# Attention with experts on one core: two heads stacked and normalised ahead of one output product of 128 rows

## The reference

```python
normed = x / l2 * dim ** 0.5 * gamma
q, k, v = split_heads(normed @ w_qkv)             # 16 heads of 64
sim = einsum('bhid,bhjd->bhij', q * d ** -0.5, k)
sim = where(causal_mask, -max, sim)
attn = softmax(sim, axis=-1)
out = einsum('bhij,bhjd->bhid', attn, v)          # (b, h, 1024, 64)
return concat_heads(out) @ w_out                  # (1024, 1024) @ (1024, 128)
```

## Time and profile before

| | |
|---|---|
| median of 3 runs | 1565.51 us (1565.09 to 1565.91) |
| the profiled execution | 1564.66 us, of which the span of the instructions is 1562.8 us |
| granted TensorE clock, mean | 0.969 of 2.4 GHz; 1.00 through the attention from 340 us to 1500 us |
| busy over the span | PE 93%, DVE 69%, ACT 68%, POOL 58% |
| 500 to 1500 us, per 200 us | PE 195 to 197, DVE 143 to 153, ACT 147 to 149, POOL 133 to 140 |

### The profile page before, as it was taken

One profiled execution on the slowest core, in us unless ns is written; L12 is line 12 of the kernel. 1 busy time (PEld: TensorE's weight loads), 2 busy tenths in 40 slices (PEclk: granted clock), 3 DMA queues, 4 the chain that ended last, 5 costly groups with the idle time before them and its releaser, 6 DMA issues.

```text
span 1562.8 us, 28739 instructions
## 1 busy us (share of the span) xinstructions
PE 1449.6 (93%) x9130; PEld 1126.8 (72%) x9131; DVE 1076.4 (69%) x2341; ACT 1067.4 (68%) x2590; POOL 907.1 (58%) x923
## 2 busy tenths in 40 slices
PE   3559999699999999999999999999999999999998
PEld 3548888467777777777777777777777777777776
DVE  6565555457776877687768776876687668866883
ACT  2445566267777777777777777777777777777775
POOL 0762000157666766676667666766676667666766
PEclk9579999689999999999999999999999999999999
DMA  9122211111111111111111111111111111111111
GB/s 311 46 79 71 58 54 52 44 35 42 33 28 38 40 33 29 38 40 33 29 38 40 33 28 40 38 33 28 39 38 33 28 41 37 33 28 42 37 28 55
DMA packets 58759, 72.34 MB, mean 46 GB/s; under 512 B 7400, under 2 KB 44560, under 8 KB 58640
## 3 DMA queue, kind: packets, MB, share of 16 engines
q1 hardware_dynamic: 40720, 52.57, 14.2%
q10 hardware_dynamic: 13824, 9.86, 2.0%
q0 software_dynamic: 4096, 8.40, 1.8%
HBM read 20.47 MB, written 16.52 MB: 24 GB/s over the span
## 4 chain that ended last, share of the span: by engine, by line
PE 66%; DVE 9%; ACT 3%; issue 2%; DMA 1%; SPq 0%; POOLq 0%; POOL 0%; DVEq 0%; ACTq 0%
PE max_ps L1291 9%; PE score_ps L1316 8%; PE score_ps L1317 8%; PE misc_ps L1350 8%; PE head_ps L1333 7%; PE head_ps L1337 7%; PE head_ps L1335 7%; PE misc_ps L1267 3%; DVE q_a L1125 3%; PE max_ps L1294 2%; PE score_ps L1319 2%; DVE row_max L1135 2%; ACT p_hi L1082 1%; PE misc_ps L1261 1%; PE misc_ps L1300 1%
## 5 line engine op out<-in xcount | busy, mean ns | idle before, releaser
L1033 POOL TENSOR_TENSOR p_lo<-probs,p_hi 128x512 fp32r<-128x512 f32 (+3 forms) x768 | 775.0, 1025 | 415.1 <-ACT p_hi L1082 408.7
L1082 ACT ACTIVATE probs<-score_ps 128x512 f32<-128x512 f32 (+3 forms) x768 | 375.4, 489 | 236.2 <-PE score_ps L1319 168.6
L1135 DVE TENSOR_REDUCE row_max<-max_ps 128x1 f32<-128x128 f32 (+7 forms) x512 | 386.7, 756 | 157.2 <-PE max_ps L1294 146.7
L1082 ACT ACTIVATE p_hi<-score_ps 128x512 fp32r<-128x512 f32 (+3 forms) x768 | 373.2, 486 | 0.0
L1333 PE MATMUL head_ps<-p_hi,v_hi 128*65 128x512 f32 (+3 forms) x768 | 295.2, 384 | 0.3 <-POOL p_lo L1033 0.3
L1316 PE MATMUL score_ps<-q_a,k_a 128*128 128x512 f32 (+3 forms) x768 | 266.6, 347 | 3.1 <-DMA q_b<-shift 3.1
L1317 PE MATMUL score_ps<-q_b,k_b 65*128 65x512 f32 (+3 forms) x768 | 266.9, 348 | 0.0
L1291 PE MATMUL max_ps<-k_a,q_a 128*128 128x384 f32 (+5 forms) x768 | 249.6, 380 | 16.4 <-DVE row_max L1135 12.6
L1337 PE MATMUL head_ps<-p_lo,v_hi 128*65 128x512 f32 (+3 forms) x768 | 258.7, 337 | 0.0
L1335 PE MATMUL head_ps<-p_hi,v_lo 128*64 128x512 f32 (+3 forms) x768 | 258.5, 337 | 0.0
L1316 PEld LDWEIGHTS score_ps<-q_a,k_a 128*128 128x128 f32 x768 | 144.8, 189 | 46.4 <-issue 3.7
(11 more groups left out here) (170 smaller groups left out, 2106.0 us busy)
## 6 DMA issues: line engine op xcount, KB each, us to landing
k_a<-k_a SPq DMA_DIRECT2D x64, 256.0 KB, 3.3
q_b<-q_a SPq DMA_DIRECT2D x64, 256.0 KB, 4.2
sorted_x<-zeros SPq DMA_DIRECT2D x13, 384.0 KB, 15.2
w_raw<-sorted_x SPq DMA_DIRECT2D x26, 192.0 KB, 2.5
sorted_y<-result ACTq DMA_DIRECT2D x78, 64.0 KB, 1.6
acc<-in_L_attn_x_dram SPq DMA_DIRECT2D x4, 512.0 KB, 9.0
w_raw<-in_L_ffn_W_dram ACTq DMA_DIRECT2D x1, 2048.0 KB, 22.7
q_b<-shift SPq DMA_DIRECT2D x128, 2.0 KB
```

The lines of the kernel that those rows point to most:

```text
L1033: pool.tensor_tensor(p_lo[:, slot, 0:w], probs[:, slot, 0:w], p_hi[:, slot, 0:w].bitcast(F32), ALU.subtract).then_inc(p_split, 1)
L1082: ins = act.activation(p[:, (g * CH + c) % RING, 0:width], score_ps[(g * CH + c) % 2][:, 0:width], ACT.Exp, scale=SCALE)
L1135: dve.tensor_reduce(row_max[:, g % 2, t:t + 1], src, axes, ALU.max).then_inc(max_taken, 1)
```

## The change

The two heads of a pair share one output product. ScalarE copies each half head, still unnormalised, with its denominator row to `raw`, which holds four half heads (two heads by two halves). The denominators, 512 numbers on one partition, go through a chain of steps, whose place is counted in chunks after the half's last chunk (`CHAIN`): SP folds them to 16 partitions by 32 (a DMA, 5 chunks later), VectorE inverts (8), SP stores the inverse to DRAM (9) and spreads it from there over 64 partitions (12), VectorE multiplies `raw` with it into rows 0 to 63 or 64 to 127 of `heads` (16). The output product then has 128 rows and 128 columns, 4 tiles to a unit, two units for a pair: at chunk 8 of the even head and chunk 4 of the odd head that follow. One addition on VectorE takes a unit to `acc`. `probs` goes from 6 slots to 4, and ScalarE waits for GpSimd's step of 4 chunks before. The walk is now one list without the split by `hp`; both programs are unrolled.

```diff
-            heads = sb(ph2, "heads", [HEAD + 1, 2, SEQ])
+            raw = sb(ph2, "raw", [HEAD + 1, 2, 2, BANK])
+            heads = sb(ph2, "heads", [P, SEQ])
-            wo = sb(ph2, "wo", [HEAD + 1, 2, D + 1])
+            wo = sb(ph2, "wo", [P, D])
+            CHAIN = [("fold", 5), ("invert", 8), ("store", 9), ("spread", 12), ("normalise", 16)]
-            Y_AT = [6, 9, 10]
-            y_units = [(0, 3), (3, 3), (6, 2)]
+            Y_AT = {8: 0, CH + 4: 1}
...
+                for kind, lag in CHAIN:
+                    if at >= lag and (at - lag) // CH < ALL_HEADS and (at - lag) % CH in LAST:
+                        order.append((kind, (at - lag) // CH, LAST.index((at - lag) % CH)))
...
+                    def fold_denominator(g, half):
+                        sp.wait_ge(raw_out, n_half(g, half) + 1)
+                        sp.dma_start(den[:, half], raw[HEAD:HEAD + 1, g % 2, half].rearrange("o (f n) -> o f n", f=FOLD)
+                                     ).then_inc(den_folded[half], 16)
+                    def store_inverse(g, half):
+                        sp.wait_ge(inverted, n_half(g, half) + 1)
+                        sp.dma_start(inv_rows[half].rearrange("(f n) -> f n", f=FOLD), inv[:, half]
+                                     ).then_inc(inv_stored[half], 16)
+                    def spread_inverse(g, half):
+                        sp.wait_ge(inv_stored[half], 16 * g + 16)
+                        sp.dma_start(scale[:, half], inv_rows[half].partition_broadcast(HEAD)
+                                     ).then_inc(scale_spread[half], 16)
...
+                            if n_chunk(g, c) >= PROBS:
+                                act.wait_ge(p_split, n_chunk(g, c) - PROBS + 1)
...
-                    def denominators(hp, g, n, u):
-                        dve.reciprocal(rden[:, u % 2, 0:tiles], src[:, :, D]).then_inc(recip_done, 1)
-                    def add_y(hp, g, n, u):
-                        for t in range(tiles):
-                            ins = dve.scalar_tensor_tensor(out=row, in0=src[:, t, 0:D], scalar=rden[:, u % 2, t:t + 1],
-                                                           in1=row, op0=ALU.mult, op1=ALU.add)
+                    def invert(g, half):
+                        dve.wait_ge(den_folded[half], 16 * g + 16)
+                        dve.reciprocal(inv[:, half], den[:, half]).then_inc(inverted, 1)
+                    def normalise(g, half):
+                        dve.wait_ge(scale_spread[half], 16 * g + 16)
+                        dve.tensor_tensor(heads[s * HEAD:(s + 1) * HEAD, cols], raw[0:HEAD, s, half], scale[:, half],
+                                          ALU.mult).then_inc(normalised, 1)
+                    def add_y(p, n, u):
+                        dve.tensor_tensor(acc[:, toks], misc_ps[u % 2][:].rearrange("p (t d) -> p t d", t=GROUP),
+                                          acc[:, toks], ALU.add).then_inc(y_added, 1)
...
-                        for t in range(tiles):
-                            ins = pe.matmul(dst[:, t * (D + 1):(t + 1) * (D + 1)], heads[:, g % 2, q0:q0 + P],
-                                            wo[:, g % 2], start=True, stop=True)
+                        pe.wait_ge(normalised, n_half(2 * p + 1, n) + 1)
+                        for t in range(GROUP):
+                            ins = pe.matmul(dst[:, t * D:(t + 1) * D], heads[:, q0:q0 + P], wo[:],
+                                            start=True, stop=True)
```

More of the change, by code:

```diff
@@ L887, in numbered @@
                 return out_
-            def misc_units(order):
-                return [o[:3] for o in order if o[0] in MISC_KINDS]
-            before_loop = ([(kind, 0, n) for n in range(6) for kind in ("project", "project_lo")]
-                           + [("max", 0, m) for m in range(PARTS)]
-                           + [("shift", 0, 0)])
-            for c in range(CUT):
-                before_loop += beside(0, c, False)
-            before_loop = numbered(before_loop, 0)
-            first_units = misc_units(before_loop)
@@ L899, in attention_and_experts @@
-            MISC0 = len(first_units)
-            def plan(last):
-                order = []
-                for at in range(CUT, G * CH + (LAG if last else CUT)):
-                    order += beside(at // CH, at % CH, last)
-                if last:
-                    order += [(kind, G - 1, n) for n in range(len(y_units)) for kind in ("y", "add")]
-                return numbered(order, MISC0)
-            MISC = len(misc_units(plan(False)))
-            assert MISC % 2 == 0
-            def n_max(hp, g, m):
-                return hp * (G * PARTS) + (g * PARTS + m)
@@ L917, in n_chunk @@
[L917 to L937 removed]
+            order = [(kind, 0, n) for n in range(6) for kind in ("project", "project_lo")]
@@ new lines, in attention_and_experts, with n_max, n_chunk, n_half @@
+            order += [("max", 0, m) for m in range(PARTS)] + [("shift", 0, 0)]
+            for at in range(ALL_HEADS * CH + 2 * CH):
+                order += beside(at)
+            order = numbered(order)
+            misc_units = [o[:3] for o in order if o[0] in MISC_KINDS]
+            def n_max(g, m):
+                return g * PARTS + m
+            def n_chunk(g, c):
+                return g * CH + c
+            def n_half(g, half):
+                return g * 2 + half
+            def n_y(p, n):
+                return p * 2 + n
@@ L994, in _ @@
-                    run(walk, sp)
+                    for kind, g, c, u in order:
+                        if kind == "shift":
+                            lay_shift(g, c)
+                        elif kind == "project" and c == 3:
+                            copies(g)
+                        elif kind == "project" and c == 5 and g % BATCH == BATCH - 1 and g + 1 < ALL_PAIRS:
+                            sp.wait_ge(misc_ready, u + 1)
+                            qkv_weights(sp, g // BATCH + 1)
+                        elif kind == "gather" and g == 0:
+                            sp.wait_ge(group_taken, c + 1)
+                            sp.dma_start(x_row[:], x_tiles[:, c * GROUP:(c + 1) * GROUP]).then_inc(x_again, 16)
+                        elif kind == "fold":
+                            fold_denominator(g, c)
+                        elif kind == "store":
+                            store_inverse(g, c)
+                        elif kind == "spread":
+                            spread_inverse(g, c)
+                        elif kind == "y" and c == 1 and g % BATCH == BATCH - 1 and g + 1 < ALL_PAIRS:
+                            sp.wait_ge(misc_ready, u + 1)
+                            out_weights(g // BATCH + 1)
@@ L1228, in _ @@
-                    run(walk, dve)
+                    for kind, g, c, u in order:
+                        if kind == "max":
+                            maximum(g, c)
+                        elif kind == "project_lo":
+                            project(g, c, u)
+                        elif kind == "weights":
+                            w_lo(c)
+                        elif kind == "invert":
+                            invert(g, c)
+                        elif kind == "normalise":
+                            normalise(g, c)
+                        elif kind == "add":
+                            add_y(g, c, u)
+                        elif kind == "gather" and g == 0:
+                            dve.tensor_copy(places[:].rearrange("p (n q) -> p n q", n=2),
+                                            slots[:, :, c * GROUP:(c + 1) * GROUP]).then_inc(group_taken, 1)
+                        elif kind == "combine":
+                            combine(c, g)
@@ new lines, in _ @@
+                    for kind, g, c, u in order:
+                        if kind == "score":
+                            score(g, c)
+                        elif kind == "max":
+                            max_scores_of(g, c)
+                        elif kind == "project":
+                            project(g, c, u)
+                        elif kind == "shift":
+                            shifts(g, c, u)
+                        elif kind == "pv":
+                            values(g, c)
+                        elif kind == "y":
+                            project_out(g, c, u)
```

344 lines of the change are left out of this document (133 added, 211 removed).

## The result

The changed kernel takes 1664.79 us (median of 4, 1664.51 to 1665.60), the one before 1565.30 beside it: a ratio of 1.064 (1.062 to 1.066), 99.5 us slower. The direction was forecast, the size was not: 1573 with a range to 1598.

What follows compares the result with a forecast made beforehand. TensorE was taken to bound the attention. Eight groups of heads gave +3.6 us and the kernel's end +4.3, together +8: 1572.5 against the profiled 1564.66, 1573.4 against the median; forecast 1573, 8-in-10 range 1538 to 1598.

Steps and rivals of the forecast that it cites:

- heads with the experts' rows: Three heads of eight in attention: VectorE is full and sets the pace; its balance of work lengthens each by 0.56 us.
- The fourth rival: Even heads: the multiply loses its turn to a second GpSimd instruction, +0.69 in three heads a group, 17 us: 1590; no separate chance.
- The group's other heads: Heads without the experts' rows, two odd and three even of eight: -0.78 us for each odd, +0.11 for each even.
- The output product: TensorE in attention: units of 1.90 us replace 3.88 a pair, 1.98 off, 63 us for 32 pairs if nothing replaces them.
- the wait of 0.39 for the maximum: Even head, chunk 8: TensorE arrives earlier and waits 0.39 us until VectorE has taken the maximum before.
- Multiply, inversion, transfers: VectorE's multiply 0.56 us plus about 0.45 waiting for GpSimd, inversion 0.35; transfers: fold 1.73, store 1.6, spread 2.3.
- The second rival: Attention: the normalising multiply does not wait for GpSimd; 28 us less, 4 more after attention: about 1542; chance 0.22.
- The third rival: Even head: the fold, late behind copies, delays VectorE's inversion and next maxima; a 5 us trip gives 1611; chance 0.17.
- The end: From ScalarE's last copy to the last store's issue: 8.8 us instead of 4.5, so +4.3.
- the last unit: Final output product on TensorE, after the last multiply: priced at 0.95 us.

## Why the prediction was wrong

**The step that failed: heads with the experts' rows.** The prediction said that there "VectorE sets the pace, and its balance is" +0.56 a head. These heads lengthened by 6.46, 0.92 and 4.29 us. Yet VectorE's busy time in them, waits for GpSimd included, rose by only 1.7, 1.5 and 1.5. Head 3 before and after (columns as in the earlier trace rows):

```profile
843.85:864.64 20.79, 19.55 (x122) 14.31 (x119) 18.65 (x46) 13.94 (x33) 13.28 (x14) 1.00 0.00 1
```

```profile
878.88:906.13 27.25, 21.99 (x114) 15.97 (x112) 20.38 (x42) 13.98 (x33) 14.46 (x15) 0.87 0.04 11
```

So what failed was to take VectorE's balance for the length of the head: VectorE is idle for 6.9 us of head 3 now, and for 2.1 before. The length comes from a chain: VectorE waits for GpSimd ahead of a maximum or a multiply that TensorE needs, TensorE stands still for up to 3.82 us and then works at the 1.2 GHz level, and VectorE waits for TensorE's next product. The balance counted VectorE's own new and lost work and half a GpSimd instruction for each multiply (head 3's took 1.70 and 1.50, not 1.01). It left out that `combine`'s old instructions wait for GpSimd too, and that GpSimd's rests would go when TensorE lost the units between its chunks. The rows were there. A multiply of `combine` took 1.13 beside GpSimd; it was used to price the new instruction and not asked of the old ones. And the window in which VectorE looked full holds a copy that takes 0.16 us with GpSimd's work cut:

```profile
843.29 1.25 DVE L1146 COPY gsc<-weights 128x8 f32<-128x8 f32 x1
```

The fourth rival had the mechanism (a turn lost to a second GpSimd instruction), but in the even heads and as the upper side of the forecast, 17 us.

**The clock was not priced.** All of the earlier trace rows stood at 1.00, and a wait was counted as long as it lasts. Waits of 2.7 and 3.8 us were followed by 3.4 and 5.1 us of work at the 1.2 GHz level.

**The group's other heads.** The output product was mis-sized: from start to start it falls from 1.71 to 0.89 us a head, 0.82 and not 0.99 (the chain of waits gives each stretch to one instruction and so counted its edges). Of the wait of 0.39 for the maximum 0.07 appeared; the unit waited 0.49 for the multiply instead of 0.71. The errors cancel, so that the sums came out near by luck: +0.2 for +0.11, -0.66 for -0.78. Head 2, with its gathers, was counted as free and lost 1.0.

**Multiply, inversion, transfers.** 0.94 came for 0.56 + 0.45, 0.33 for 0.35. The second rival (no waiting) is out: alone the multiply takes 0.67. The row that it rested on shows a wait as well, on the other engine: the subtraction beside the addition of 744.62 took 1.86 us instead of 1.29.

```profile
744.60 1.86 POOL L1033 TENSOR_TENSOR p_lo<-probs,p_hi 128x512 fp32r<-128x512 f32 x1 [0.79 <-ACT p_hi L1082]
```

The Trainium skill (SBUF — State Buffer, "SBUF: two separate sides") says that of the two engines whichever starts first has the shared ports for its whole instruction. The rows of the steps agree: they end 0.03 to 0.09 us after GpSimd's instruction. By the starts on record two rows do not: the addition of 744.62 and the multiply of 937.04 begin 0.02 and 0.25 us after GpSimd's subtraction, and it was the subtraction that waited. The third rival did not come: VectorE idled 4.9 us ahead of its inversions between 400 and 1600 us.

**The end** cost 6.2 us, not 4.3. From the last copy to the last store's issue (timeline of ACT, DVE, SP and PE), answering to the earlier trace rows:

```profile
1648.62 0.59 ACT L1091 ACTIVATE raw<-head_ps 65x512 f32<-65x512 f32 x1 [2.67 <-PE head_ps L1326]
...
1650.95 0.34 DVE L1182 RECIPROCAL inv<-den 16x32 f32<-16x32 f32 x1 [2.77 <-DMA den<-raw]
...
1655.65 0.68 DVE L1188 TENSOR_TENSOR heads<-raw,scale 64x512 f32<-64x512 f32 x1 [0.72 <-DMA scale<-inv_rows]
...
1658.57 0.69 DVE L1195 TENSOR_TENSOR acc<-misc_ps,acc 128x512 f32<-128x512 f32 x1 [2.23 <-PE misc_ps L1336]
1659.29 0.38 SPq L996 DMA_DIRECT2D out_dram<-acc  x1
```

```profile
1656.48 2.05 PE L1336 MATMUL misc_ps<-wo,heads 128*128 128x128 f32 x8 [2.28 <-DVE heads L1188]
```

```profile
1656.00:1659.00 3.00, 2.05 (x8) 1.78 (x8) 0.77 (x2) 0.00 (x0) 0.00 (x0) 0.50 1.02 296
```

The fold took 1.74 (1.73 assumed), the store and the spread 4.36 together (3.9). The term that was mis-sized most is the last unit, 2.05 for 0.95: TensorE had stood for 2.28 us ahead of it, and the granted clock was 0.50.

## What to carry to other kernels

When work is taken from the engine that sets the pace, ask what the others did in the time it took: here the time of the removed matrix products had been GpSimd's rests, and part of VectorE's instructions on SBUF ran in them. An engine that is nearly full does not set the length by its sum of work; ask what the other engines wait for, and what stands ahead of it. Price every instruction of VectorE that meets GpSimd, not only the new ones, and place such steps where both engines rest. A stall of some microseconds on TensorE is to be priced with the slow stretch that follows it.

## What the runs showed of the hardware

A VectorE copy of 128x4 between SBUF tiles waited out three GpSimd instructions that stood ready one behind the other (3.39 us; 0.16 with GpSimd's work cut), while the four steps at 937.58 got a turn after each. What decides between the two was not found. A VectorE multiply whose record begins 0.25 us after that of a GpSimd subtraction took 0.62, and the subtraction 1.55 instead of 0.74. GpSimd's 64x512 multiply took 1.27 us where VectorE's alone took 0.67.
